# Row maxima of an attention block: one reduction per two tiles, or one multiplication per tile that accumulates a minimum

## What is computed

```
q = Wq @ ln(x);  k = Wk @ ctx;  v = Wv @ ctx            # per batch: 128x1024, 128x256, 128x256
energy = q.T @ k / sqrt(128)                            # 1024 x 256
x = x + Wskip @ ln(x) + (softmax(energy, axis=-1) @ v.T).T
w = (nibbles(qweight) - round(zeros / scales).T) * scales.T     # 1024 x 1024
x = x + ln(x) @ w + bias
```

## Time and profile before

| | us |
|---|---|
| median of 3 runs | 517.02 (516.99 to 517.34) |
| the profiled execution | 517.71 |
| its span, first to last instruction | 515.6 |
| PE busy | 496.5 (96%) |
| POOL busy | 467.1 (91%) |
| DVE busy | 435.3 (84%) |
| ACT busy | 376.8 (73%) |
| TensorE's granted clock, mean | 1.000 |

### The profile page before, as it was taken

One profiled execution on the slowest core, in us unless ns is written; L12 is line 12 of the kernel. 1 busy time (PEld: TensorE's weight loads), 2 busy tenths in 40 slices (PEclk: granted clock), 3 DMA queues, 4 the chain that ended last, 5 costly groups with the idle time before them and its releaser, 6 DMA issues.

```text
span 515.6 us, 9359 instructions
## 1 busy us (share of the span) xinstructions
PE 496.5 (96%) x2672; PEld 299.4 (58%) x2672; DVE 435.3 (84%) x1001; ACT 376.8 (73%) x867; POOL 467.1 (91%) x711
## 2 busy tenths in 40 slices
PE   4888999999999999999999999999999999999987
PEld 3544456665666656566665566666556666565644
DVE  4989898888988888898888889888889888887752
ACT  4889778777787777778777777877777877777520
POOL 4786999999999999999999999999999999999763
PEclk9999999999999999999999999999999999999999
DMA  8774678778968987887878786787767687757653
GB/s 305 204 156 108 183 176 157 204 187 187 197 171 202 156 199 183 196 182 179 211 150 193 185 206 176 180 204 156 196 178 197 172 202 190 168 130 145 167 130 120
DMA packets 227203, 92.65 MB, mean 180 GB/s; under 512 B 209488, under 2 KB 214352, under 8 KB 227152
## 3 DMA queue, kind: packets, MB, share of 16 engines
q1 hardware_dynamic: 226432, 91.91, 73.9%
q10 hardware_dynamic: 720, 0.14, 0.2%
HBM read 23.87 MB, written 16.78 MB: 79 GB/s over the span
## 4 chain that ended last, share of the span: by engine, by line
PE 83%; POOL 8%; issue 3%; DVE 3%; ACT 2%; DMA 1%; POOLq 0%; ACTq 0%; SPq 0%
PE ps_y L1020 38%; PE ps_e L974 15%; PE ps_o L1015 13%; PE ps_o L1009 7%; PE ps_kv L992 2%; PE ps_y L1026 2%; PE ps_kv L988 2%; POOL sb_prob L273 2%; POOL sb_xn_lo L318 2%; PE ps_e L970 1%; POOL sb_o L267 1%; DMA sb_x<-in_x_dram 1%; ACT sb_prob L506 1%; POOL sb_rstd L281 1%; DVE sb_neg_max L697 1%
## 5 line engine op out<-in xcount | busy, mean ns | idle before, releaser
L1020 PE MATMUL ps_y<-sb_wf,sb_xnt_hi 128*128 128x512 f16 x496 | 188.3, 380 | 3.3 <-DMA sb_xnt_lo<-sb_xn_lo 3.3
L1020 PE MATMUL ps_y<-sb_wf,sb_xnt_lo 128*128 128x512 f16 x496 | 188.0, 379 | 0.0
L506 ACT ACTIVATE sb_prob<-ps_e,sb_neg_max 128x256 f32<-128x256 f32 x256 | 118.2, 470 | 51.5 <-DVE sb_neg_max L697 51.4
L273 POOL TENSOR_SCALAR sb_prob<-sb_prob,sb_rsum 128x256 f32<-128x256 f32 x256 | 122.5, 492 | 7.3 <-DVE sb_rsum L702 7.2
L706 DVE TENSOR_TENSOR sb_p_lo<-sb_prob,sb_p_hi 128x1024 f16<-128x1024 f32 x64 | 78.1, 1220 | 36.5 <-ACT sb_p_hi L515 36.4
L267 POOL TENSOR_TENSOR sb_o<-sb_prod,sb_x 128x512 f32<-128x512 f32 x63 | 84.9, 1348 | 5.8 <-DVE sb_prod L740 5.8
L697 DVE TENSOR_REDUCE sb_neg_max<-ps_e 128x2 f32<-128x512 f32 x128 | 85.0, 682 | 1.8 <-PE ps_e L970 1.4
L515 ACT ACTIVATE sb_p_hi<-sb_prob 128x1024 f16<-128x1024 f32 x64 | 67.4, 1053 | 23.3 <-issue 23.3
L1020 PEld LDWEIGHTS ps_y<-sb_wf,sb_xnt_hi 128*128 128x128 f16 x496 | 48.4, 98 | 61.0 <-DMA sb_xnt_lo<-sb_xn_lo 4.3
L1020 PEld LDWEIGHTS ps_y<-sb_wf,sb_xnt_lo 128*128 128x128 f16 x496 | 48.5, 98 | 54.8
L974 PE MATMUL ps_e<-sb_k_hi,sb_xc_hi 128*128 128x256 f32 x224 | 78.6, 351 | 0.1
(11 more groups left out here) (150 smaller groups left out, 976.0 us busy)
## 6 DMA issues: line engine op xcount, KB each, us to landing
sb_x<-in_x_dram SPq DMA_DIRECT2D x32, 512.0 KB, 3.9
out_dram<-sb_o SPq DMA_DIRECT2D x63, 256.0 KB, 2.4
sb_ctx<-in_ctx_dram SPq DMA_DIRECT2D x32, 128.0 KB, 2.7
sb_q<-in_L_ffn_qweight_dram SPq DMA_DIRECT2D x4, 512.0 KB, 7.5
sb_pt_hi<-sb_p_hi SPq DMA_TRANSPOSE x64, 3.0
sb_pt_lo<-sb_p_lo SPq DMA_TRANSPOSE x64, 2.9
sb_scale_row<-in_L_ffn_scales_dram SPq DMA_DIRECT2D x1, 512.0 KB, 9.6
sb_xnt_hi<-sb_xn_hi SPq DMA_TRANSPOSE x32, 2.8
```

The lines of the kernel that those rows point to most:

```text
L273: last = pool.tensor_scalar(prob[:, b % 2, j, t, :], prob[:, b % 2, j, t, :], rsum[:, j, t:t + 1], P_SCALE, ALU.mult, ALU.mult)
L506: done = act.activation(prob[:, b % 2, j, t, :], ps_e[j % 2][:, t, :], ACT.Exp, bias=neg_max[:, j, t:t + 1], accum_out=esum[:, j, t:t + 1])
L1020: pe.matmul(ps_y[h][:, :], xnt_p[s][:, q % 2, kt, :], wf[:, kt, h * HALF:(h + 1) * HALF], start=kt == 0 and s == 0, stop=False)
```

## The change

`row_max` no longer reduces a chunk at once. For each of the two tiles it multiplies the energies by -1 and accumulates the minimum of the products in `neg_max[:, j, t]`; since min(-e) = -max(e), the value is the same. The products, 128x256 fp32, are written to the slot of `prob` that `exps(b, j)` overwrites afterwards. A batch has eight TENSOR_SCALAR in place of four TENSOR_REDUCE; the semaphore `max_done[j]` is raised by the second of a chunk. Nothing is moved: the order of everything else on all engines is as before, and lines behind L698 move down by two.

```diff
             def row_max(b, j):
                 dve.wait_ge(scores_done[j], b + 1)
-                dve.tensor_reduce(neg_max[:, j, :], ps_e[j % 2][:, :, :], AX.X, ALU.max,
-                                  negate=True).then_inc(max_done[j], 1)
+                for t in range(TPC):
+                    last = dve.tensor_scalar(prob[:, b % 2, j, t, :], ps_e[j % 2][:, t, :], -1.0, None, ALU.mult, ALU.min,
+                                             accum_out=neg_max[:, j, t:t + 1])
+                last.then_inc(max_done[j], 1)
```

## The result

The changed kernel takes 518.43 us (median of 11 runs, 517.48 to 519.21) against 517.05 for the kernel before (11 runs, 516.82 to 517.46): a ratio of 1.0024 with a 95% interval of 1.0016 to 1.0033. The profiled execution took 518.16 us, with a span of 516.0.

A forecast was written before the change was run, and what follows sets the result against it. PE bounds the kernel at 15.14 us a step; +0.24 us a chunk lifts DVE's loop from 14.71 to 15.67. 26 x 0.53 = 13.8, less 0.4, plus 2.0 outside gives 15.4 and 532.4 us (+3.0%), range 517.5 to 552.

The forecast's parts named there:

- What bounds the kernel: Steady part: PE is busy throughout, 15.14 us a step over 26 periods; a DVE change can only lose.
- The multiplications: Row maxima on DVE: each 256-element multiplication holds DVE 0.33 us, two 0.66 against 0.60 for the reduction replaced.
- The accumulator read: DVE, eight more instructions a step: each read costs 0.09 us, taken from ACT's row, making a chunk +0.24 us.
- rival 1: Not slower: accumulator read on DVE nearly free, chunk +0.06 us, PE still sets 15.14, 517.4 us; chance 0.13.
- The bound of 0.00: Lower bound for the accumulator read on DVE: if free it costs 0, and a chunk +0.06 us.
- the threshold of +0.11: Row maxima on DVE: up to 0.11 us of added work a chunk is hidden by the loop's slack.
- The loop of 14.71 us and its hole: DVE from one variance to the next needs 14.71 us, including 4.09 us waiting through POOL and ACT before p_lo.
- The 1.29 us of idle time: DVE's idle time ahead of p_lo is no room: a later variance makes p_lo later by the same.
- The slack: DVE's loop hides 0.43 us a step: 0.10 before chunk 0's maximum and 0.33 before L666.
- PE's wait: PE would wait about 0.5 us a step for ACT's exps before the scores of chunk 3.
- the rival between forecast and serial case: Accumulator reads on DVE at 0.15 to 0.20 us, chunk +0.36 to +0.46, 540 to 552 us; chance 0.13.
- serial case: DVE reads and multiplications wait for each other, chunk +0.52 to +0.62 us, about 563 to 573 us; chance 0.08.

The follow-up runs named there:

- the kernel with one column: The changed kernel with one one-column DVE instruction added behind each chunk's maxima; 539.94 us, 1.0436 to the kernel before.
- the kernel with one more reduction: The changed kernel with one more 256-wide reduction ahead of each chunk's multiplications; 552.09 us, 1.0670 to the kernel before.
- that with three: The changed kernel with three one-column DVE instructions added behind each chunk's maxima; 547.14 us, 1.0576 to the kernel before.
- the column behind the inverse: The changed kernel with one one-column DVE instruction per chunk, chunk 3's placed behind its inverse instead of before stats2; 525.05 us, 1.0151 to the kernel before.
- the two parts: Multiplications only in batches 5 to 30 (steady part), reductions elsewhere: 518.06 us; the converse, multiplications only in batches 0 to 4 and 31: 518.08 us.

## Why the prediction was wrong

- **What bounds the kernel** held: PE's 15.14 us a step, nothing to gain for DVE, only to lose.
- **The multiplications** held: 0.34 us from start to start, taken as 0.33.
- **The accumulator read** is the step that failed. Its count held (256), its price did not: 0.09 us was taken from ACT's row (271.16 to 271.25), and it is 0.00 on DVE. With it the chunk costs +0.08 and not +0.24, and the loop comes to 14.71 + 0.32 = 15.03 us and not 15.67. The prediction had this as its rival 1, with the point from which it decides at 0.025 us a read, and gave it 0.13. The bound of 0.00 was in the sum; the value was picked because the ACT row is the same operation, on another engine. The argument against, that even a one-column instruction costs its successor 0.08 us, compared the read with an instruction of another kind: in the kernel with one column the column costs 0.06 us and the read right in front of it nothing (270.39 for both, next start 270.45). The chunk's +0.08 stayed under the threshold of +0.11. That 518.43 us lies inside the stated range of 517.5 to 552 is no merit of the sum: the lower end was set by the edge of this rival.
- **The loop of 14.71 us and its hole** held as a mechanism: the kernel with one more reduction was expected at 551 to 555 us and took 552.09, though with a period 0.1 us shorter than expected and more time outside the 26 periods, so its hitting the range is in part luck. The 1.29 us of idle time ahead of p_lo was no room in any kernel.
- **The slack** was a little over-stated. The prediction set the next variance at 275.42, which is 260.28 + 15.14; the row stands at 275.49, so that step alone would have given 14.78 us. The mean over 24 steps is 14.76, which makes the threshold (15.14 - 14.76) / 4 = 0.10 us a chunk, and single steps have less (0.07 at 14.88). The change sits near that edge; that this is why the steady part costs 0.9 us and not nothing is likely, but not shown.
- **What was not seen** is the collision of p_lo with POOL's rstd. Had the read cost 0.09 us, the time would probably not have been 532 but between the 540 us of the kernel with one column (0.14 us a chunk over the reduction) and the 547 of that with three (0.26). This is an estimate from these two kernels; it takes for granted that such a read would have put p_lo in front of rstd as a column does, which no run shows. The rows of before showed it: nb, one column wide, takes 0.75 us against rstd's 0.55, though it is no more work; the kernels in which p_lo doesn't overlap it show 0.26 for the same instruction. The prediction took both as fixed durations.
- **PE's wait** ahead of the scores of chunk 3 is absent in the changed kernel (0.3 us, once) and grew with what was added to the chunks: 0.7 us with the column behind the inverse, 13.4 with one column, 18.9 with three, 23.5 with one more reduction.
- **The sum of the rival between forecast and serial case** was off: +0.36 to +0.46 a chunk gives loops of 16.15 to 16.55 us and, added up like the forecast, about 545 to 555 us, not 540 to 552. Nothing hangs on it here.
- **Rival 1's time**, 517.4, was 1.0 us short: it had PE's period as a hard floor and six chunks outside, and the runs show 0.9 us for each of the two parts.

## What to carry to other kernels

Idle time of an engine is room only if what ends it does not wait for that engine itself: walk round the loop from one instruction back to the same one, and count the part that runs through other engines as time that DVE can't fill. A price of 0.09 us taken from another engine's row, where 0.025 decides, doesn't make a chance of 0.84 for slower against 0.13 for the same; where the price of one instruction decides between two cases, its own bounds set their chances. And before durations on POOL are added up as constants, look at what DVE does beside them: which one starts first can be worth more than the work that is added.

## What the runs showed of the hardware

- A DVE multiplication from PSUM with an accumulator output shows as TENSOR_SCALAR_CACHE_REDUCE, 418 ns for 128x256, and a DVE_READ_ACCUMULATOR of 83 ns, whose successor starts in the same hundredth of a microsecond. On ACT the next exp starts 0.09 us behind the start of such a read the earlier trace rows.
- Two 256-wide instructions from PSUM cost 0.66 (reductions) to 0.68 us (multiplications with accumulator), one of 512 costs 0.60.
- A POOL instruction that reads SBUF is held up by a DVE subtraction with both inputs in SBUF (128x1024) that is ahead of it: a one-column power on POOL took 0.55 us when it started 0.04 us or more ahead, and 1.62, 1.60 and 1.52 us when it started 0.01 ahead, 0.01 behind and 0.09 behind, each time ending 1.61 us behind the subtraction's start. Two 256-wide multiplications took 2.17 us instead of 0.93.
- Two one-column DVE instructions a step, 0.12 us, cost 10.7 us of 517 in one place and 0.5 in another.
